# An adaLN block with attention and a routed FFN on one core: activation tables named by hand, one wait moved, instruction orders searched anew

## What is computed

```
mod = (silu(c) @ wmod) -> sa, ca, ga, sb, cb, gb         # per sequence, 256 wide each
h = layernorm(x) * (1 + ca) + sa
x = x + ga * attn(h)            # scores = |q k^T| / 16, causal, softmax, @ v, @ Wo^T + bo
h = layernorm(x) * (1 + cb) + sb
x = x + gb * ffn(h)
ffn(h): cluster = argmax(calibrate(h @ cluster_sigs.T)); tile = argmax over the cluster's 8 tiles
        comp = tanh(gelu(h @ w1 + b1) @ w2 + b2)           # exact gelu, 2 numbers per token
        mag  = relu(comp @ spline_w1[tile] + spline_b1[tile]) @ spline_w2[tile] + spline_b2[tile]
        y    = layernorm(h + mag * directions[tile] * 0.1) * gamma + beta
```

## Time and profile before

| | before |
|---|---|
| median of 3 runs | 487.49 us (486.3 to 489.53) |
| profiled execution | 487.89 us |
| its span, first to last instruction | 486.1 us |
| TensorE busy, share of the span | 403.8 us, 83% |
| VectorE busy | 364.5 us, 75% |
| ScalarE busy | 343.9 us, 71% |
| GpSimd busy | 76.9 us, 16% |
| mean granted clock of TensorE | 0.927 |

### The profile page before, as it was taken

How to read it: one execution, slowest core, us unless ns; L and a number is a source line. 1 busy time by engine, 2 the same in 40 slices (tenths; PEclk the granted TensorE clock), 3 DMA queues, 4 the chain that set the end, 5 groups by cost and what they waited for, 6 DMA issues and landing times.

```text
span 486.1 us, 7764 instructions
## 1 busy us (share of the span) xinstructions
PE 403.8 (83%) x2080; PEld 312.1 (64%) x2080; DVE 364.5 (75%) x1334; ACT 343.9 (71%) x726; POOL 76.9 (16%) x111
## 2 busy tenths in 40 slices
PE   4999999499999999899889997999699967716130
PEld 4867767468587877587668675769477755615120
DVE  3684573267949886798888887888888759787797
ACT  1346728268997599878987897789768976856720
POOL 4135100610201200000500051002400200111323
PEclk9999999889999999999999998999899989966555
DMA  8610269536633740413982378444930610251574
GB/s 227 202 47 23 69 122 172 80 61 138 95 49 84 127 96 1 91 63 65 139 167 66 65 124 168 81 41 85 133 44 1 108 24 1 41 91 26 83 135 103
DMA packets 40298, 42.99 MB, mean 88 GB/s; under 512 B 3600, under 2 KB 35840, under 8 KB 40256
## 3 DMA queue, kind: packets, MB, share of 16 engines
q1 hardware_dynamic: 24752, 26.88, 24.1%
q0 software_dynamic: 14928, 14.82, 21.9%
q10 hardware_dynamic: 576, 0.80, 0.5%
HBM read 26.70 MB, written 23.13 MB: 103 GB/s over the span
## 4 chain that ended last, share of the span: by engine, by line
PE 66%; ACT 12%; issue 11%; DVE 8%; POOL 1%; DMA 1%; ACTq 0%; DVEq 0%; POOLq 0%
PE bank L606 12%; PE bank L589 12%; PE bank L566 10%; PE bank L579 9%; PE bank L628 6%; PE bank L554 3%; PE bank L597 3%; ACT L1075 3%; PE bank L615 2%; ACT L1213 2%; PE bank L668 2%; ACT gath L1225 2%; ACT y L1233 1%; DVE y L2075 1%; DMA wide<-in_L_wmod 1%
## 5 line engine op out<-in xcount | busy, mean ns | idle before, releaser
L606 PE MATMUL bank<-v,probsT 128*128 128x257 f32 x320 | 83.7, 397 | 12.6 <-issue 11.2
L589 PE MATMUL bank<-h,g 128*128 128x128 f32 (+3 forms) x256 | 80.6, 444 | 0.0
L606 PEld LDWEIGHTS bank<-v,probsT 128*128 128x128 f32 x320 | 60.7, 198 | 26.3 <-issue 17.3
L579 PE MATMUL bank<-m_ga,h 128*128 128x258 f32 x256 | 66.9, 385 | 4.4 <-ACT hidT L1208 3.8
L566 PE MATMUL bank<-h,a_sb 128*128 128x512 f32 x128 | 59.6, 593 | 0.0
L1797 POOL DMA_DIRECT2D out<-y x14 | 18.0, 1285 | 261.8 <-DVE y L2099 261.8
L579 PEld LDWEIGHTS bank<-m_ga,h 128*128 128x128 f32 x256 | 45.8, 192 | 15.7 <-issue 5.0
L589 PEld LDWEIGHTS bank<-h,g 128*128 128x128 f32 x256 | 44.2, 195 | 16.1 <-issue 9.4
L1141 ACT ACTIVATE bank<-bank,v 128x128 f32<-128x128 f32 (+1 forms) x64 | 31.7, 498 | 24.5 <-PE bank L589 24.1
L1924 DVE CUSTOM_DVE_ANT_0 probs<-bank,cmask 128x128 f32<-128x128 f32 (+1 forms) x64 | 30.9, 484 | 24.2 <-ACT bank L1141 23.8
L1918 DVE TENSOR_TENSOR v<-bank,a_row 128x258 f32<-128x258 f32 x64 | 26.4, 417 | 21.0 <-PE bank L579 21.0
(11 more groups left out here) (181 smaller groups left out, 857.8 us busy)
## 6 DMA issues: line engine op xcount, KB each, us to landing
x<-in_L_attn_x SPq DMA_DIRECT2D x16, 512.0 KB, 3.7
out<-gate_rows SPq DMA_DIRECT2D x14, 512.0 KB, 9.8
out<-x POOLq DMA_DIRECT2D x14, 512.0 KB, 9.1
out<-y POOLq DMA_DIRECT2D x14, 512.0 KB, 6.4
gb_row<-gate_rows SPq DMA_DIRECT2D x16, 256.0 KB, 3.9
a_row<-gate_rows SPq DMA_DIRECT2D x14, 256.0 KB, 3.3
out<-res SPq DMA_DIRECT2D x2, 512.0 KB, 2.9
wide<-in_L_wmod SPq DMA_DIRECT2D x1, 768.0 KB, 12.9
```

What stands on the lines that cost most here:

```text
L579: last = mm(ps[:, 0:VW], h[s][:, c, t * P:(t + 1) * P], m_ga[p % 2][s][:, c, :], start=(c == 0), stop=(c == KC - 1))
L589: last = mm(ps[:, 0:w], g[s][:, c, t * P:(t + 1) * P], h[s][:, c, 0:w], start=(c == 0), stop=(c == KC - 1))
L606: last = mm(ps[:, 0:D + 1], probsT[s][t][:, j * P:(j + 1) * P], v_sb[s][:, j, 0:D + 1], start=(j == 0), stop=(j == t))
```

## The change

Five things are edited.

1. `gelu_table()` is new and names Gelu's set. It stands in ScalarE's list ten times, each time behind the last exp ahead of a Gelu or Tanh. `tanh` no longer names a table; `exp_table()` stands behind the last Gelu or Tanh ahead of the next exp, ten times, and once at the start as before.
2. In `y_nw` the wait for `yhat_rdy` moves from i = 0 to i = 2, the instruction that overwrites `rstd`.
3. The orders of all five engines are other ones.
4. The banks are dealt anew.
5. On GpSimd the jobs are interleaved differently, and on SyncE the late gate rows are sent one step earlier.

```diff
-            "AT13 CM G11 PT03 PT13 S10 S13 su_col",
...
+            "CM G01 G11 GA5 S10 S13 su_A su_gb",
...
             def exp_table():
                 nc.scalar.preload_act_table_set("natural_log_exp_and_others")
+
+            def gelu_table():
+                nc.scalar.preload_act_table_set("gelu_and_others")
...
                 A(comp[g % 2][:, 0:tiles(g), :], cmp_t[:, 0:tiles(g), :], ACT.Tanh).then_inc(tanh_rdy, 1)
-                exp_table()
...
             def y_nw(g, i):
                 if i == 0:
                     dve.wait_ge(ln3_guess, g + 1)
+                if i == 2:
                     need(dve, yhat_rdy, NT * before(min(g, BY_DVE)))
...
# SyncE
             for i in range(0, 2):
                 ldga(1, i)
-            for i in range(0, 2):
-                ldga(2, i)
+            ldga(2, 0)
+            dma_gb()
+            ldga(2, 1)
             ldx(2, 0)
-            dma_gb()
-            ldx(2, 1)
...
# GpSimd
-            ms(2, 0)
+            ax(0, 0)
             sp_sig()
-            ms(2, 1)
+            for i in range(0, 2):
+                ms(2, i)
+            sp_rest()
             ms(3, 0)
-            ax(0, 0)
-            sp_rest()
             ax(0, 1)
...
```

More of the change, by code:

```diff
@@ L722, in _ @@
+            S_(0, 1, 1)
+            su_gb()
+            PT_(0, 0, 3)
+            S_(0, 1, 2)
+            for i in range(2, 4):
+                V_(0, 1, i)
+            AT(0, 0, 2)
+            XT(1, 0, 0)
+            PT_(0, 1, 0)
+            AT(0, 0, 3)
+            XT(1, 0, 1)
+            XT(1, 1, 0)
+            PT_(0, 1, 1)
+            S_(0, 1, 3)
+            AT(0, 1, 0)
+            V_(1, 0, 0)
+            G_(1, 0, 0)
+            PT_(0, 1, 2)
+            for i in range(1, 3):
                 AT(0, 1, i)
-            XT(1, 1, 0)
@@ L866, in _ @@
-            for i in range(1, 4):
                 GA(1, i)
@@ new lines, in _ @@
+            b_g(1, 0, 0)
+            a_h(1, 1, 1)
+            b_g(1, 0, 1)
+            c_gs(0)
+            b_abs(1, 0, 0)
+            for i in range(0, 3):
+                c_xh(0, i)
+            b_exp(1, 0, 0)
+            b_abs(1, 0, 1)
+            b_exp(1, 0, 1)
+            c_xh(0, 3)
+            b_abs(1, 0, 2)
+            c_xh(0, 4)
+            b_g(1, 1, 0)
+            b_exp(1, 0, 2)
+            b_abs(1, 0, 3)
+            b_pt(1, 0, 0)
+            for i in range(5, 8):
+                c_xh(0, i)
@@ L1579, in _ @@
[L1579 to L1588 removed]
+            b_pt(7, 0, 0)
+            b_exp(7, 0, 1)
+            yh(3, 7)
+            c_xh(6, 0)
+            b_pt(7, 0, 1)
+            for i in range(1, 6):
+                c_xh(6, i)
+            b_abs(7, 0, 2)
@@ L2366, in _ @@
+            b_st(1, 1, 1)
+            a_st(3, 0, 0)
+            loc(0, 1)
+            b_ri(1, 1, 2)
+            b_x2(1, 1, 2)
+            loc(0, 2)
+            for i in range(1, 3):
+                a_st(3, 0, i)
+            loc(0, 3)
             b_st(1, 1, 2)
@@ new lines, in _ @@
+            for i in range(3, 5):
+                loc(1, i)
+            c_var(2, 0)
+            y_(0, 5)
+            y_st(0, 2)
+            for i in range(1, 3):
+                c_var(2, i)
+            y_st(0, 3)
+            c_var(2, 3)
+            y_(0, 6)
+            b_v(3, 0, 1)
+            c_b2(1)
+            for i in range(0, 4):
+                c_nw(2, i)
+            y_st(0, 4)
+            b_v(3, 0, 2)
+            for i in range(5, 7):
+                loc(1, i)
+            a_st(4, 0, 3)
@@ new lines, in _ @@
+            b_x2(7, 1, 2)
+            y_st(5, 6)
+            clc(7, 5)
+            yg(4, 5)
+            clc(7, 6)
+            b_ri(7, 1, 3)
+            clc(7, 7)
+            c_b2(6)
+            b_x2(7, 1, 3)
+            y_st(5, 7)
+            clc(7, 8)
+            yg(4, 6)
+            clc(7, 9)
+            y_var(5, 0)
+            clb(7, 0)
+            y_var(5, 1)
+            clb(7, 1)
+            for i in range(2, 4):
+                y_var(5, i)
+            yg(4, 7)
+            for i in range(1, 4):
+                b_st(7, 1, i)
@@ L2965, in _ @@
             clc(8, 7)
-            y_nw(6, 1)
+            yg(5, 4)
             for i in range(8, 10):
                 clc(8, i)
+            clb(8, 0)
+            c_b2(7)
+            clb(8, 1)
+            y_nw(6, 1)
+            clb(8, 2)
+            yg(5, 5)
+            clb(8, 3)
+            spl(7, 0)
+            clb(8, 4)
+            c_b2(8)
+            for i in range(0, 2):
+                pick(8, i)
+            spl(7, 1)
+            yg(5, 6)
+            for i in range(2, 4):
+                spl(7, i)
@@ L3036, in _ @@
-            spl(8, 5)
+            yg(6, 6)
+            for i in range(4, 6):
+                spl(8, i)
+            yg(6, 7)
             for i in range(0, 3):
```

2184 lines of the change are left out of this document (1044 added, 1140 removed), and 14 rows, old and new, of the table BANK.

## The result

The changed kernel takes **474.38 us** (median of 4 runs, 473.61 to 476.03), the kernel before 488.51 beside it: ratio 0.972, 95% interval 0.967 to 0.977, so 2.8% faster. The forecast was 464, the range 454 to 477. The time lies in the range, and 10 us above the forecast. The profiled execution took 473.61 us, its span is 471.8.

What follows compares the result with a forecast made beforehand. TensorE was taken as the bound from 95 to 392 us, VectorE and ScalarE in the tail; joints 10.5, start 7.5 and tail 6 sum to 24 off 487.9, forecast 464 us, range 454 to 477.

Steps and rivals of the forecast that it cites:

- three signs of being wrong: GpSimd's first send released after 72 us, ScalarE idle over 20 us before h copies, or VectorE over 95% in loop windows.
- TensorE over 24 of 25 us busy from 70 to 95: Sign that would show the start's gain, beside no cluster exp wait for the FFN table over 1 us.
- The joints: Between pairs, 190 to 392 us: fewer table loads free probsT's copy and TensorE; 10.5 us, 60% of a 17.6 us bound.
- rival A: Waits move: start mended, but ScalarE idles before the h copy at joints and half the other gains go; 472 us, 23%.
- The tail: From 392 us on: norm 3's first Newton steps no longer wait for yhat; 6 us, between 0 and 12.
- The start: 70 to about 102 us: earlier FFN table ends the cluster exp's wait, TensorE's idle time and slow clock; 7.5 us.
- The setup: First 70 us: setup products change places, bias columns may wait before A for GpSimd's loads; counted 0, ±2 us.
- D: Slower: GpSimd's queue delays signatures and scaled M, decided if sequence 0's beta rows land after 78.5 us; 499 us, 5%.

Runs made afterwards that it cites:

- named_wait_table_early: Kernel before, in its order and banks, with Gelu's set named (21 loads), the yhat wait at the third Newton step and the FFN table built early: 460.08 us.
- beta_bias: Changed kernel with sequence 0's beta row and sequence 5's x load sent earlier, and TensorE's bias columns behind A, Wo's transposes and a gate row: 460.23 us.
- x_first: Changed kernel with the x load of sequence 5 back directly behind that of sequence 4, ahead of the beta and gb rows: 469.74 us.
- named_wait_old_order: Kernel before, in its order, banks and queues, with Gelu's set named (21 loads) and the yhat wait at the third Newton step: 472.04 us.
- one_beta_first: Changed kernel with SyncE sending sequence 0's first beta row, then sequence 5's x load, ahead of the gb and other beta rows: 463.12 us.

## Why the prediction was right, and where not

The time lies in the stated range, and in part that is luck: of four terms two failed, and the range, which was to reach from one rival to behind another, was wide enough for it. None of the three signs of being wrong showed itself (GpSimd's first send was released at 70.80, ScalarE's idle time before the h copies is 5.9 us, VectorE is busy for 179.92 of 202.00 us), since none of them looked at the x load; only "TensorE over 24 of 25 us busy from 70 to 95" did, with 15.00 measured.

*The joints (10.5 forecast, 11.2 measured).* Right in mechanism and size. The number of loads is 21 and 26.9 us, exp to exp took 5.4 us for 5.3, the period of a pair is 46.5 us (x2 of sequence 7, 9 and 11 at 215.4, 261.9, 308.4), within 46 to 48, and no clock under 0.9 is left there. The 60% of the bound of 17.6 us was read from no row, so that 11.2 came for 10.5 is luck in the size. The share of the loads is settled: 8.0 of the 11.2 come in the old order too, by 12 loads fewer, and the new order adds 3.2; with 33 loads the new order gives 4.6. That ScalarE would wait for the h copy (rival A) didn't come: 5.9 us in all instead of the 14.3 of the earlier trace rows.

*The tail (6 forecast, 8.4 measured).* Right in sign, a little low, and its cause is shown only in part. The moved wait gives 3.6 us by the medians when it is alone and 1.9 on top of the tables. Twelve loads fewer give 2.5 in the tail of the new order (117.2 to 114.7), which the forecast had counted in the joints alone. How much is the order's no run shows: in the old order named_wait_table_early has a tail of 114.4 us, as short as that of the new one, and the tail also hangs on the granted clock (see the last section).

*The start (7.5 forecast, 0.0 measured).* **This step failed**, and the sentence in it is that "their send stands ahead of the x load of 54.39, and behind that load nothing waits for the second sequence any more". I saw the x load of sequence 5 leave its place and counted only what it no longer held back. I did not ask where it went (behind seven large rows), nor who waits for it (VectorE's statistics, with row maxima and the temperature queued behind them). The rest of the step was nearly right: beta was issued at 59.5 and not 55, landed at 70.8 and not 65, and the cluster exp did not wait for the table. With the load mended the stretch gains 10.6 us, more than the 7.5; together with the setup, up to x2 of sequence 6, it is 5.7 (194.5 for 200.2), and 8.3 with the bias columns mended too (191.9).

*The setup (0 ± 2 forecast, −5.4 measured).* The second step that failed. I had seen that "the bias columns stand before A and can wait there for GpSimd's loads" and took it that the products behind would need the time anyway. beta_bias shows 2.1 us of loss there by x2 of sequence 1, 2.9 us by the medians. The other 3.3 may be work that was put ahead of that x2; whether any of it is lost, no run shows.

*The rivals.* A's 472 is near the time, but for another reason: A has the start mended and the joints half lost, and it was the other way round. D, slower, had the right place, GpSimd's send waiting for beta, and in x_first, where it is released at 81.98, past the 78.5 that D named, it does cost TensorE 5.45 us. In the changed kernel it was released at 70.80. *The sum*: 24 forecast; 14.3 in the spans. 24 less the 7.5 and 5.4 that failed, and 0.7 and 2.4 more than forecast in loop and tail, is 14.2.

## What to carry to other kernels

When an order changes, follow each transfer that moves in both directions: what it no longer holds back, and who waits for it in its new place; then count the bytes under way at the moment it is issued, on all queues. Before searching orders anew, mend the named causes one by one: here three local edits in the old order (name the set that serves both functions, build a table before the step that waits for memory, move one wait) gave 460.1 us, where the whole change as it came gave 474.4. A gain of a searched order should be looked at by stage, since two lost stages were hidden in a faster sum.

## What the runs showed that I had not expected

*The clock in the tail.* named_wait_old_order and named_wait_table_early have the same order on all engines behind the start, yet the last 4.9 us between them arise in the tail. These are windows of 4 us at the same place of the program, first of the one and then of the other:

```profile
392.00:396.00 4.00, 2.43 (x10) 1.89 (x10) 3.93 (x12) 3.74 (x9) 0.00 (x0) 0.66 0.01 4
396.00:400.00 4.00, 4.00 (x21) 3.80 (x20) 2.93 (x13) 1.53 (x3) 0.00 (x0) 0.50 0.00 0
```

```profile
384.00:388.00 4.00, 2.42 (x12) 1.66 (x13) 3.96 (x13) 3.74 (x9) 0.00 (x0) 1.00 0.00 0
388.00:392.00 4.00, 3.04 (x27) 2.83 (x26) 3.90 (x14) 2.82 (x5) 0.00 (x0) 1.00 0.02 4
```

TensorE had idled alike in both (2.6 of 4 us busy in the window ahead, and the same two standstills, 1.40 and 1.48 us long, in its rows):

```profile
391.38 0.67 PE L606 MATMUL bank<-v,probsT 128*128 128x257 f32 x2 [1.40 <-ACT probsT L1155]
...
394.39 2.05 PE L606 MATMUL bank<-v,probsT 128*128 128x257 f32 x4 [1.48 <-issue]
```

```profile
384.01 0.67 PE L606 MATMUL bank<-v,probsT 128*128 128x257 f32 x2 [1.40 <-ACT probsT L1155]
...
387.02 1.11 PE L606 MATMUL bank<-v,probsT 128*128 128x257 f32 x4 [1.48 <-issue]
```

In the first the granted clock fell to 0.50, its lower level of 1.2 GHz, from about 393.5 to 406.5 us, and in the second it stayed at 1.00. The changed kernel shows the fall too (0.50 from 395 to 401 us). One of the four runs of named_wait_old_order took 467.7 us at a mean clock of 0.940, the other three 471.9 to 472.4 at 0.932 and 0.933. So 4 to 5 us of the tail hang on something that the order alone doesn't set; what decides it stays open, and I would not claim the 4 us beyond additivity for any edit.

*Slow matmuls at full clock.* In one_beta_first four bias matmuls of one column took 0.98 us behind the standstill at 11.95; in beta_bias the same four, behind A, took 0.50. The granted clock is 1.00 in both, so it does not explain the difference, and the cause is open.

*VectorE beside GpSimd.* The long multiply of the earlier trace rows (4.03 us) shrank to 1.59, but the stall only moved, as the prediction had feared: L1980, whose median is 0.18 us, takes 2.41 while GpSimd sends y and scales M.

```profile
240.07 2.41 DVE L1980 TENSOR_SCALAR cal<-cal 128x64 f32<-128x64 f32 x1
```

It was in the chain twice, at 240 and 287 us; TensorE idled 0.58 us behind the first, and that is the most that this one can have cost it.
